# GELU in two instructions, the general softmax path as a loop, and the cross decision ahead of the last value products of self-attention

## What is computed

```python
h = _layernorm(x, ln1_g, ln1_b)
x = x + _mha(h, h, sa_wq, sa_bq, ...)              # self-attention, 2048 keys
h = _layernorm(x, ln2_g, ln2_b)
x = x + _mha(h, context, ca_wq, ca_bq, ...)        # cross-attention, 1601 keys
h = _layernorm(x, ln3_g, ln3_b)
h = jax.nn.gelu(h @ mlp_w1.T + mlp_b1, approximate=False) @ mlp_w2.T + mlp_b2
return x + h
```

## Time and profile before

| | us |
|---|---|
| median of 3 runs | 1489.96 (1488.52 to 1492.16) |
| profiled execution | 1488.8 |
| its span | 1487.1 |
| PE busy | 1387.4 (93%) |
| ACT busy | 1096.3 (74%) |
| DVE busy | 591.0 (40%) |

### The profile page before, as it was taken

One profiled execution on the slowest core, in us unless ns is written; L12 is line 12 of the kernel. 1 busy time (PEld: TensorE's weight loads), 2 busy tenths in 40 slices (PEclk: granted clock), 3 DMA queues, 4 the chain that ended last, 5 costly groups with the idle time before them and its releaser, 6 DMA issues.

```text
span 1487.1 us, 20712 instructions
## 1 busy us (share of the span) xinstructions
PE 1387.4 (93%) x8014; PEld 630.7 (42%) x8014; DVE 591.0 (40%) x1377; ACT 1096.3 (74%) x1354; POOL 47.4 (3%) x70
## 2 busy tenths in 40 slices
PE   7989989998679999999999998999999999999987
PEld 5668776786322223223223322322333333433347
DVE  5556675676730223313323231441441243144133
ACT  3544334445469999999999988889887798788843
POOL 2000000000110000000000000000000000000000
PEclk9999999999889999999999999999998999999999
DMA  9410001001385000000000353601000000000000
GB/s 302 158 46 1 1 0 57 1 12 41 117 160 90 23 12 12 26 28 23 26 26 14 45 118 48 155 29 46 14 12 15 22 12 12 22 15 1 5 11 15
DMA packets 35047, 66.05 MB, mean 44 GB/s; under 512 B 6202, under 2 KB 20092, under 8 KB 34204
## 3 DMA queue, kind: packets, MB, share of 16 engines
q1 hardware_dynamic: 29580, 43.24, 13.0%
q0 software_dynamic: 5360, 21.37, 3.9%
HBM read 42.70 MB, written 22.02 MB: 44 GB/s over the span
## 4 chain that ended last, share of the span: by engine, by line
PE 76%; ACT 13%; DVE 7%; issue 4%; DMA 1%; DVEq 0%; SPq 0%; ACTq 0%
PE PS L1461 25%; PE PS L1444 18%; ACT PX L992 10%; PE PS L1543 3%; PE PS L1511 2%; PE PS L1228 2%; PE PS L1231 2%; PE PS L1492 2%; PE PS L1241 2%; PE PS L1190 1%; PE PS L1191 1%; PE PS L1192 1%; PE PS L1526 1%; PE PS L1494 1%; PE PS L1493 1%
## 5 line engine op out<-in xcount | busy, mean ns | idle before, releaser
L992 ACT ACTIVATE PX<-PS 128x1024 f32<-128x1024 f32 (+1 forms) x928 | 880.0, 1101 | 123.7 <-PE PS L1444 84.5
L1461 PE MATMUL PS<-PX,V 128*32 128x512 f32 (+1 forms) x3712 | 501.8, 613 | 11.9 <-DVE OT L2126 8.0
L1444 PE MATMUL PS<-QST,stack 50*128 50x512 f32 (+1 forms) x1856 | 382.9, 472 | 18.8 <-issue 13.8
L1444 PEld LDWEIGHTS PS<-QST,stack 50*128 50x128 f32 (+1 forms) x1856 | 155.9, 186 | 410.8 <-ACT PX L992 332.5
L1461 PEld LDWEIGHTS PS<-PX,V 128*32 128x32 f32 (+1 forms) x3712 | 74.0, 108 | 161.7 <-issue 113.6
L2126 DVE COPY OT<-PS 128x512 f32<-128x512 f32 x32 | 22.1, 692 | 217.5 <-PE PS L1461 216.1
L823 ACT ACTIVATE PH<-PS 128x512 fp32r<-128x512 f32 (+1 forms) x52 | 31.2, 600 | 80.0 <-PE PS L1171 69.2
L1543 PE MATMUL PS<-W,HIDT 128*128 128x256 f32 x192 | 51.7, 415 | 9.7 <-ACT HIDT L976 9.7
L2161 DVE RECIPROCAL REC<-REC 128x256 f32<-128x256 f32 x30 | 52.6, 1753 | 1.0
L1543 PEld LDWEIGHTS PS<-W,HIDT 128*128 128x128 f32 x192 | 36.7, 201 | 35.3 <-issue 30.8
L841 ACT ACTIVATE TR<-PS,small 128x128 f32<-128x128 f32 x32 | 10.0, 364 | 51.1 <-PE PS L1231 51.1
(11 more groups left out here) (220 smaller groups left out, 1577.4 us busy)
## 6 DMA issues: line engine op xcount, KB each, us to landing
QST<-q_parts SPq DMA_DIRECT2D x192, 64.0 KB
q_parts<-PARTS POOLq DMA_DIRECT2D x16, 512.0 KB, 3.3
stack<-k_parts SPq DMA_DIRECT2D x24, 200.1 KB, 6.5
stack<-k_parts SPq DMA_DIRECT2D x18, 256.0 KB
k_parts<-KPARTS POOLq DMA_DIRECT2D x8, 512.0 KB, 3.2
v_cross<-V POOLq DMA_DIRECT2D x1, 3328.0 KB, 13.1
V<-v_cross SPq DMA_DIRECT2D x2, 1664.0 KB, 12.9
k_parts<-PARTS POOLq DMA_DIRECT2D x6, 512.0 KB, 3.4
```

Of the source, the lines that this page charges most:

```text
L992: act.activation(exp_place(a, h)[0:kr, :, :], PS[0:kr, slot:slot + 2, :], ACT.Exp, scale=SCALE).then_inc(at["exp"], 1)
L1444: ins = pe.matmul(PS[0:kr, score_slot(a, h) + jj, :], KST[a][lo:lo + NROW, pair, kt * P:kt * P + kr].bitcast(F32R), QST[lo:lo + NROW, pair ...
L1461: ins = pe.matmul(PS[32 * j:32 * j + 32, 6, :], V[0:kr, kt, 2 * (g // 2 * GH + j) + g % 2, :], exp_place(a, 2 * (c * steps + t) + j // 2)[ ...
```

## The change

The general path becomes a loop over groups on PE and DVE. For that, its queries and keys are loaded to one fixed place for each group (keys are loaded once more for each group), and the semaphore `max` starts at 1. Nothing of this runs when the bound holds, apart from the jump. The GELU becomes two instructions of half the width, and the `o` parts wait for the half that they read. The table puts all four parts of the first `o` tile into step 37 and the rest into every second step. At the end of self-attention the decision and the first cross scores come ahead of the last value products. The value load of the last two groups stands behind the cross decision on SP's queue.

```diff
-     "o": [37, 37, 39, 39, 42, 42, 43, 43, 45, 45, 46, 46, 48, 48, 49, 49]},
+     "o": [37, 37, 37, 37, 39, 39, 41, 41, 43, 43, 45, 45, 47, 47, 49, 49]},
...
+            def load_values(g, last):
+
+                sp.wait_ge(A[0]["pv"], last)
+                sp.dma_start(V[:, 0:LT, (g - 1) * GH:(g + 1) * GH, :],
+                             vd.rearrange("p (k h e) -> p k h e", k=LT, h=HEADS)
+                             [:, :, (g - 1) * GH:(g + 1) * GH, :]).then_inc(s_vst[g // 2], 16)
...
-                    if g % 2:
-
-                        sp.wait_ge(A[0]["pv"], last)
-                        sp.dma_start(V[:, 0:LT, (g - 1) * GH:(g + 1) * GH, :],
-                                     vd.rearrange("p (k h e) -> p k h e", k=LT, h=HEADS)
-                                     [:, :, (g - 1) * GH:(g + 1) * GH, :]).then_inc(s_vst[g // 2], 16)
+                    if g == 1:
+                        load_values(g, last)
...
             else:
-                sp.wait_ge(A[0]["pv"], HALVES // 2)
+                load_values(GROUPS - 1, HALVES // 2)
                 sp.dma_start(W1[:], d["w1T"].rearrange("(c p) n -> p c n", p=P)).then_inc(S["w1_loaded"], 16)
...
             def gelu(q):
 
-                act.wait_ge(at["unit_taken"], HID // P * (q + 1))
-                act.activation(HIDT[:], HIDT[:], ACT.Gelu).then_inc(at["gelu"], 1)
+                w = HID // P // 2
+                for half in range(2):
+                    act.wait_ge(at["unit_taken"], HID // P * q + w * (half + 1))
+                    act.activation(HIDT[:, half * w:(half + 1) * w], HIDT[:, half * w:(half + 1) * w], ACT.Gelu) \
+                        .then_inc(at["gelu"], 1)
...
                 def one(c):
-                    for g in range(GROUPS):
-                        pe.wait_ge(G[f]["q"], 16 * QLOADS * (c * GROUPS + g + 1))
+                    with pe.Fori(0, GROUPS) as g:
+                        pe.wait_ge(G[f]["q"], (c * GROUPS + g) * (16 * (QLOADS + KLOADS)) + 16 * (QLOADS + KLOADS))
                         for j in range(GH):
+                            lo = (j % 2) * HALF
                             for tt in range(TPC):
-                                if g or j or tt:
-
-                                    pe.wait_ge(G[f]["max"], (c * GROUPS + g) * GH * TPC + j * TPC + tt)
-                                lo, pair = (j % 2) * HALF, 2 * g + j // 2
+                                pe.wait_ge(G[f]["max"], (c * GROUPS + g) * (GH * TPC) + (j * TPC + tt + 1))
...
-            def pv(c, t):
+            def pv(c, t, a=a, at=at, NK=NK, steps=steps):
...
                 if kind == "o":
-                    if first:
-                        pe.wait_ge(at["gelu"], q + 1)
+                    if part % 2 == 0:
+                        pe.wait_ge(at["gelu"], 2 * q + 1 + part // 2)
...
                     if t == 0:
+                        if a == 1 and first:
+                            self_pv(CHUNKS - 1, GROUPS * NKS[0] - 1)
                         if not first:
                             pv(c - 1, steps - 1)
...
+            if a == 0:
+                self_pv = pv
+                continue
             pv(CHUNKS - 1, steps - 1)
-            if a == 0:
-                continue
             sums(CHUNKS, 0)
```

More of the change, by code:

```diff
@@ L547, in _, with load_q @@
             steps = GROUPS * NKS[a]
-            def load_q(c, g, s_to):
+            def load_q(c, g, s_to, place=None):
+                pair = 2 * (g if place is None else place)
                 for b, part in enumerate(QBLOCK):
@@ L553, in load_q @@
                         at_ = odd * HALF + b * HD
-                        sp.dma_start(QST[at_:at_ + HD, 2 * g:2 * g + 2, :], rows[odd]).then_inc(s_to, 16)
+                        sp.dma_start(QST[at_:at_ + HD, pair:pair + 2, :], rows[odd]).then_inc(s_to, 16)
             def load_shift(c, g, s_to):
@@ L612, in general, with load_staged_keys @@
                 bounded = sp.value_load(flag[0:1, f:f + 1], min_val=0, max_val=1)
+                def load_staged_keys(g):
+                    for b, part in enumerate(KBLOCK):
+                        rows = kd[a][part, g * GH * HD:(g + 1) * GH * HD, :] \
+                            .rearrange("(j two d) n -> two d j n", two=2, d=HD)
+                        for odd in range(2):
+                            at_ = odd * HALF + b * HD
+                            sp.dma_start(KST[a][at_:at_ + HD, 0:2, 0:KEYS[a]], rows[odd]).then_inc(G[f]["q"], 16)
                 def one(c):
                     for g in range(GROUPS):
-                        if g:
-                            sp.wait_ge(G[f]["max"], (c * GROUPS + g) * GH * TPC)
-                        load_q(c0 + c, g, G[f]["q"])
+                        sp.wait_ge(G[f]["max"], (c * GROUPS + g) * GH * TPC + 1)
+                        load_q(c0 + c, g, G[f]["q"], 0)
+                        load_staged_keys(g)
                     sp.wait_ge(G[f]["split"], c + 1)
@@ L624, in general @@
                 with sp.If(bounded < 1):
+                    for i in range(len(s_kst[a])):
+                        ones = 2 if a == 0 and i in (0, CHUNKS, CHUNKS + 1, CHUNKS + 2) else 0
+                        sp.wait_ge(s_kst[a][i], 16 * (KLOADS + ones))
                     wait_parts_stored(sp, (1 + a) * CHUNKS + c0 + n)
@@ L1412, in general @@
                     pe.wait_ge(G[f]["split"], n_chunks)
[L1413 to L1415 removed]
+                    pe.wait_ge(G[f]["q"], 16 * (GROUPS * (QLOADS + KLOADS) * n_chunks + KLOADS
+                                                + (GROUPS * QSLOADS if f < 2 else 0)))
                 if f == 1:
@@ L1420, in _, with scores @@
             general(a)
-            def scores(c, n, first):
+            def scores(c, n, first, a=a, at=at, NK=NK, steps=steps):
                 h = c * steps * 2 + n
@@ L2093, in one @@
                     gch.base, gch.n = c, 0
-                    for g in range(GROUPS):
+                    with ve.Fori(0, GROUPS) as g:
                         for j in range(GH):
                             for tt in range(TPC):
-                                n = (c * GROUPS + g) * GH * TPC + j * TPC + tt
-                                ve.wait_ge(G[f]["scores"], n + 1)
-                                ve.tensor_reduce(sm(MX + tt * HEADS + g * GH + j), flat[:, 0:KEYS[a]], AX,
-                                                 ALU.max, negate=True).then_inc(G[f]["max"], 1)
+                                n = (c * GROUPS + g) * (GH * TPC) + (j * TPC + tt + 1)
+                                ve.wait_ge(G[f]["scores"], n)
+                                ve.tensor_reduce(small[:, bass.ds(g * GH + (MX + tt * HEADS + j), 1)],
+                                                 flat[:, 0:KEYS[a]], AX, ALU.max, negate=True) \
+                                    .then_inc(G[f]["max"], 1)
                                 ve.wait_ge(G[f]["max"], n + 1)
```

10 lines of the change are left out of this document (5 added, 5 removed).

## The result

The changed kernel takes 1469.05 us (median, 1466.65 to 1476.99), the kernel before 1491.06 in the same comparison (1488.52 to 1493.18): a ratio of 0.9862, 95% interval 0.9821 to 0.9903. The prediction was 1467. The gain of 22.0 us between the medians stands beside the 22.9 of the prediction. The profiled execution took 1468.47 us.

A forecast was written before the change was run, and what follows sets the result against it. The prediction saw a PE and ACT lockstep losing time to long PE jumps and GELU waits. Terms 3.95 + 4.6 + 3.6 + 2.7 + 6.3 + 1.7 = 22.9 us gave 1465.9, 1467 as median; range 1459 to 1481.

The forecast's parts named there:

- distance against two packets: PE's three decision jumps stall only when the target lies beyond the packet being read and the next.
- VectorE's 0.06: At PE's decisions, the cost in us assumed for each shortened jump, taken from VectorE's jump over its own copy.
- The rival that a jump stalls whatever its length: At PE's three decisions, shortening would not cure the stalls; total 1481 us, chance 0.14.
- Self decision, 3.95: Ahead of self-attention's first scores, PE's jump falls from 4.01 to 0.06 us, gaining 3.95.
- Cross decision, 4.6 and 0.7 of clock: Between self and cross attention, shorter jump and earlier decision gain 4.6 us; fewer slow-clock steps behind it give 0.7.
- the forecast 0.4: At the cross decision, us given back because the last value products now come before the second scores.
- Last decision, 3.6 and 2.0 of clock: After the first cross chunk, all ACT idle time goes, 3.6 us; no clock fall behind it gives 2.0.
- GELU, 6.3: In three cross chunks, second-layer parts run under the GELU's second half: about 2.1 us each, 6.3 in all.
- The 2.1 of the prediction: Gain in us per GELU chunk from one fewer step with second-layer parts and even spacing of the rest.
- Clock behind the GELU, 1.7: Behind the GELU, a 3.4 us clock fall goes in about half the cases, counted as 1.7 us.
- The late value load: Rival: values of groups 2 and 3 land late and the first cross chunk waits; slower, chance 0.02.

The follow-up runs named there:

- e2: Changed kernel with PE's loop body holding two groups, so 321 instructions to jump over instead of 176: 1478.29 us.
- e9: Changed kernel with the GELU in four instructions and six second-layer parts in step 37: 1465.24 us.
- e1: Changed kernel with PE's general path written out again over the four groups, some 605 instructions to jump over: 1480.32 us.
- e4: Changed kernel with one GELU instruction and the old table of second-layer parts: 1474.62 us.
- e7: Kernel before with only the general path made a loop; old decision order, one GELU instruction, old table: 1478.8 us.
- e5: Changed kernel with one GELU instruction but the new table, four second-layer parts in step 37: 1472.58 us.
- e6: Changed kernel with the GELU in two instructions but the old table, two parts in step 37: 1482.86 us.
- e3: Changed kernel with the last value products of self-attention ahead of the cross decision again: 1468.66 us.
- e8: Changed kernel run again without any edit, as yardstick on another chip: 1468.66 us.
- e10: Changed kernel with the cross decision's product in step 61 and the jump ahead of the value products before the last: 1468.68 us.

## Why the prediction was right

- *The jump.* The mechanism, distance against two packets, held in all 39 jumps of the thirteen profiles (eight took 3.3 to 4.1 us, 31 took 0.31 to 0.37), and e2 separates it from "any shorter jump" and from "any jump". The size was off: 0.33 us stay where the step took VectorE's 0.06, 0.3 for each of three jumps. Why PE's short jump is five times VectorE's stays open. The rival that a jump stalls whatever its length fell at once.
- *Self decision, 3.95.* From the flag's end to the first scores 3.65 us went, the 0.3 of the jump less. In the pair of profiles it does not show in the span, because the start stage was 3.3 us longer.
- *Cross decision, 4.6 and 0.7 of clock.* Near in number, other in its parts. The decision product stood 1.8 us earlier against the exponentials, as forecast, and the first cross exponential 4.9. But of this 1.7 went back at the second exponential, not 0.4, because the last value products ran at 1.2 GHz: from the last self exponential to the second cross step it is 6.76 us against 9.99, a gain of 3.2, which is the jump's 3.0 and little more. e9, where they ran at 2.4 GHz, has the forecast 0.4. The clock then gave back more than the 0.7: steps 2 to 4 took 5.94 us against 7.58, for it was low for a shorter time. At the end of the fourth step the gain is 4.9, where the prediction's terms make 5.3. That the two errors nearly cancel is luck.
- *Last decision, 3.6 and 2.0 of clock.* 3.5 and 2.2. Both e1 and e2, whose jump is long there, have the slow steps again.
- *GELU, 6.3.* 2.5 for each chunk by place (e4 against the changed kernel), 7.5 in all; 6.0 in medians. The 2.1 of the prediction is what is left when the clock does not fall (2.2 in e7's second chunk); 0.3 to 0.5 a chunk is a short fall behind the whole GELU that the prediction did not count. ACT's stores of scores sufficed, the seven exponentials behind it had no gap. Why it holds is narrower than the prediction said: e5 and e6 show that split and table each need the other. Alone the table gives 0.2 to 0.5 us a chunk and the split 0.1.
- *Clock behind the GELU, 1.7.* All of the 3.4 went. But e4, with the old wait of 3.25 us, had short falls alone, and e7 one chunk with none and one with a longer one (0.51 in 1254 to 1261), so the long fall comes and goes with a whole GELU too, and that all of it went is in part luck. Of the twelve whole GELUs in the profiles (before, e4, e5, e7) eleven have a fall behind them; of the eighteen with the changed split and table (after, e1, e2, e3, e8, e10) one has, in e10. That fits the shorter wait as the cause, but e6, with the same wait, fell for longer, so the wait alone does not settle it.
- *Not in the sum:* a clock fall at the start of the third cross chunk (first four steps 9.87 us against 8.56, granted 0.77 there; e8 has it too), 1.1 us won inside self-attention, 1.5 lost in the tail and a start 3.3 later, the last three not the change's. The terms as measured at their places (3.65, 4.9, 3.5, 2.2, 7.6 for the GELU against the kernel before, 3.4) make 25.2, against 22.9 forecast; less 3.3, 1.3 and 1.5, plus 1.1 it is 20.2, and the span shows 20.3. So the prediction's total came out the nearer by what it did not name.
- *The late value load* did not happen. It was issued at 932.25, 4.9 us earlier than before, as PE was, and no value product of group 2 waits for a DMA.

The timeline of the changed kernel, SP's queue behind the cross flag:

```profile
932.25 0.57 SPq L567 DMA_DIRECT2D V<-v_cross  x1
```

## What to carry to other kernels

Look for waits whose releaser is "issue" behind a branch, and count the instructions that it jumps over: code that is never executed costs microseconds when it lies between, and a loop, or any body that ends within the next packet (some 256 instructions on PE), took them away here. Work that waits for one long instruction of another engine wants both the instruction split and enough work placed to fill the second half; one without the other gave 0.2 to 0.5 us a chunk of 2.5 (e5), or 0.1 at best and a loss of 2.8 where the clock fell (e6). When a total varies by more than the term sought, compare the distance between two instructions on both sides of the place.

## What was not expected of the hardware

- A jump of one length costs 0.34 or 3.7 to 4.1 us (e2), and its place in the packet tells which. If that is the cause, an edit anywhere ahead of it on PE can bring or remove a stall; no run tried it.
- A taken short jump takes 0.31 to 0.37 us on PE and 0.06 to 0.07 on VectorE (all profiles).
- Behind two waits of 1.5 and 2.1 us around 2 us of work PE fell to 1.2 GHz in two chunks of three (e6), and each of these falls cost 3.1 us; the third chunk, with the same waits, had none. One wait of 3.25 us brought falls in all chunks of e4 too, but shorter ones, which cost 0.3 to 0.5 us.
- Falls of the clock come at places that an edit does not touch: the first four steps of the first cross chunk took 9.45 us in the changed kernel, 10.63 in e9 and 11.84 in e6, all with the same code ahead of them.
- The same code ahead of self-attention ends within a range of 8 us (421.3 to 429.0) from execution to execution.
